# Where the expert's number is read, and when token numbers are made, in the last eleven tiles of a mixture-of-experts kernel

## The chip, the core and the metric

The kernel runs on one core of a Trainium2 chip. The metric is the device time of one execution in microseconds, as the median of several runs. The profile is of one execution.

## What is computed

The model is one gated cross-attention layer followed by a mixture of experts. `x` is 8 x 512 tokens of width 256. The part that matters here is the second one, cut from the reference:

```
logits = einsum('btd,de->bte', layernorm(x), gate_w)      # 8 experts
top_v, top_i = top_k(logits, 2); top_w = softmax(top_v)
for e in range(8):
    h = gelu(xf @ w1[e] + b1[e])                          # 256 -> 1024, exact gelu
    out = out + comb[:, e] * (h @ w2[e] + b2[e])          # 1024 -> 256
x = x + tanh(g_ffn) * out
```

Each token goes to two of the eight experts, so which rows an expert sees is known only when the kernel runs.

## The kernel before

The rows of the tokens are first sorted into one queue per expert in DRAM. The work is then cut into 39 tiles (`N_TILES`): 32 full ones of 256 rows (`N_FULL`) and seven narrow ones of 128 rows, numbers 32 to 38, for what is left over in the experts' queues. Small tables that VectorE makes at run time hold, for each tile, the number of its expert (`expert_of`) and its place in the queue. The weights of all experts lie in the on-chip memory, split into a high and a low bf16 part (`w1_split`, `w2_split`).

The first six tiles (`EARLY`) are interleaved with the last batch of the attention, in an order written out by hand. The rest is run by `over_tiles`: tiles 6 and 7 written out, tiles 8 to 27 in a hardware loop of two tiles a turn, tiles 28 to 38 written out again. `i` is a Python integer in a written-out tile and a register in the loop; `s` is the buffer of two that the tile uses.

Every engine has its own program, kept in step by semaphores. For one tile:

- SyncE (`load`) brings the rows of tile i + 2.
- TensorE first transposes tile i + 1 (`turn`, line 2548), then does layer 1 of tile i (`all_layer1`, line 2562: 48 matmuls over three products of high and low parts), then layer 2 of tile i - 1 (`all_layer2`, line 2578: 48 matmuls in four pieces for a full tile, 24 in two pieces for a narrow one). There is one accumulator for layer 2 (the program's `ps_y`, named `ps_o` in the profile), so layer 2 of tile i - 1 waits until VectorE has added the bias of tile i - 2 out of it (`y_biased`); it also waits for `h_lo_ready`.
- ScalarE casts the transposed rows (`split_x`) and applies gelu (`gelu`).
- VectorE takes the rows' tails, weights and low parts (`prepare`, `low`) and then does `finish` for tile i - 1: bias added into `y` (line 2534), then multiplied by the row's weight (line 2537).
- GpSimd (`add`) waits until the add of tile i - 1 has landed and until `y` is weighted, makes the token numbers of the tile (`token_f`, line 2469, and `token_at`, line 2471), and issues the indirect DMA that adds the rows of `y` to the output (line 2473), one for each 128 rows.

The number of the tile's expert is read from memory into a register of the engine's sequencer by `load_expert` (line 2424), and the address of each weight block is worked out from it in registers. TensorE calls it in `all_layer1` and again in `all_layer2`; VectorE in `prepare` and in `finish`, there behind the waits:

```
dve.wait_ge(y_summed, i + 1)
if not first(i, 2):
    after_add(dve, i - 2, early)
e = load_expert(dve, i)
```

Of the kernel before, what the change touches and what calls it, by code (L numbers as in the profile page):

```python
# [3 lines left out]
P = 128  # L4
# [20 lines left out]
N_FULL, N_HALF = 2 * B * L // TILE, E - 1  # L25
N_TILES, N_ENTRIES = N_FULL + N_HALF, N_FULL + N_HALF + 2
# [7 lines left out]
EARLY = 6  # L34
# [3 lines left out]
F32, BF16, I32, U32 = (mybir.dt.float32, mybir.dt.bfloat16, mybir.dt.int32, mybir.dt.uint32)  # L38
# [188 lines left out]
def program(nc, x, ctx_t, g, wq_t, wkv_t, wc_t, gate_w, w1, b1_t, w2, b2, out):  # L227
# [11 lines left out]
    with ExitStack() as whole:  # L239
# [45 lines left out]
        general_select(nc, k, sem, sb, ps, general[0])  # L285
        general_attend(nc, k, sem, sb, ps, general[1])
        experts(nc, k, sem, sb, ps, pipeline, general)


# [2098 lines left out]
def experts(nc, k, sem, sb, ps, pipeline, general):  # L2388
    with ExitStack() as own:
# [8 lines left out]
        weight = sb(own, "weight", [P, N_TILES, 2])  # L2398
        part_a, part_b = sb(own, "part_a", [P, 2]), sb(own, "part_b", [P, 2])
        bias = [sb(own, f"bias{s}", [P, FC]) for s in range(2)]  # L2400
        token_f, token_at = sb(own, "token_f", [P, 2]), sb(own, "token_at", [P, 2], I32)
        x_hi, x_lo, ps_x, ps_h, ps_y = k.x_hi, k.x_lo, k.ps_x, k.ps_h, k.ps_y

        bias_loaded, x_turned = sem("bias_loaded"), sem("x_turned")
# [1 line left out]
        tail_taken, x_hi_ready, x_lo_ready = sem("tail_taken"), sem("x_hi_ready"), sem("x_lo_ready")  # L2406
        h_ready, gelu_done, h_lo_ready = sem("h_ready"), sem("gelu_done"), sem("h_lo_ready")
        y_summed, y_biased, y_weighted, added = sem("y_summed"), sem("y_biased"), sem("y_weighted"), sem("added")
# [4 lines left out]
                    y_biased, y_weighted)  # L2413

        all_met, pads_placed = sem("all_met"), k.pads_placed

        def first(i, n=1):
            return isinstance(i, int) and i < n

        def slot_of(i, s):  # L2420
            return (i % 2, i // 2) if isinstance(i, int) else s

        def load_expert(engine, i):
            return engine.value_load(k.expert_of[0:1, bass.ds(i, 1)], min_val=0, max_val=E - 1)

        def width(i):
            return P if isinstance(i, int) and i >= N_FULL else TILE

        def loaded(i, s, half):
            again = isinstance(i, int) and i >= N_FULL - 1 and s == (N_FULL - 1) % 2  # L2430
            return row_loaded[s], 16 * (half + (2 if again else 1))
# [21 lines left out]
        def after_add(engine, i, early):  # L2453
            if isinstance(i, int) and i < EARLY - 1:
                done, before = early
                engine.wait_ge(done, before + 32 * (i + 1))
            elif width(i) == P:
                engine.wait_ge(added, 32 * (N_FULL + 1 - EARLY) + 16 * (i + 1 - N_FULL))
            else:
                engine.wait_ge(added, 32 * (i + 2 - EARLY))  # L2460

        def add(pool, chain, i, at=None, early=(added_early, 0)):
            g = nc.gpsimd
            s, _ = slot_of(i, at)
            some = width(i) // P
            if not first(i):
                after_add(pool, i - 1, early)
            pool.wait_ge(y_weighted, i + 1)
            chain.then(g.tensor_tensor(token_f[:, 0:some], tails[:, bass.ds(i, 1), 0:some, 3].rearrange("p a s -> p (a s)"),  # L2469
                                       k.ones_f[:, 0:some], ALU.mult))  # L2470
            chain.then(g.tensor_copy(token_at[:, 0:some], token_f[:, 0:some]))  # L2471
            for t in range(some):
                pool.indirect_dma_start(k.out_rows, bass.IndirectOffsetOnAxis(ap=token_at[:, t:t + 1], axis=0),  # L2473
                                        y[s][:, t, :], None, bounds_check=B * L - 1, oob_is_err=False,
                                        compute_op=ALU.add).then_inc(early[0] if first(i, EARLY - 1) else added, 16)

# [46 lines left out]
        def finish(dve, i, at=None, early=(added_early, 0)):  # L2523
            v = nc.vector
            s, _ = slot_of(i, at)
            if first(i):
                dve.wait_ge(bias_loaded, 32)
            dve.wait_ge(y_summed, i + 1)
            if not first(i, 2):
                after_add(dve, i - 2, early)  # L2530
            e = load_expert(dve, i)
            some = width(i) // P
            b2_own = b2_all[:, bass.ds(e, 1), :].to_broadcast([P, some, D])
            v.tensor_tensor(y[s][:, 0:some], ps_y[:, 0:some], b2_own, ALU.add).then_inc(y_biased, 1)  # L2534
            dve.wait_ge(y_biased, i + 1)
            for t in range(some):
                last = v.tensor_scalar(y[s][:, t, :], y[s][:, t, :],  # L2537
                                       weight[:, bass.ds(i, 1), t:t + 1].rearrange("p a s -> p (a s)"), None, ALU.mult)
            last.then_inc(y_weighted, 1)

        def turn(pe, i, at=None):
            s, half = slot_of(i, at)
            pe.wait_ge(*loaded(i, s, half))
            if not first(i):
                pe.wait_ge(x_lo_ready, i)
            for kt in range(KT):
                for t in range(width(i) // P):
                    last = nc.tensor.transpose(ps_x[:, kt, t * P:(t + 1) * P], xg[s][:, t, kt * P:(kt + 1) * P], k.ident[:])  # L2548
            last.then_inc(x_turned, 1)
# [17 lines left out]
        def layer2(pe, i, n, at=None, e=None):  # L2567
            s, _ = slot_of(i, at)
            e = load_expert(pe, i) if e is None else e
            if n == 0:  # L2570
                pe.wait_ge(h_lo_ready, PAIRS * (i + 1))
                if not first(i):
                    pe.wait_ge(y_biased, i)
            t, some = n // 2, range((n % 2) * FC // 2, (n % 2 + 1) * FC // 2)
            token = slice(t * P, (t + 1) * P)
            terms = [(f, hs, part) for f in some for hs, part in ((h_hi, 0), (h_hi, 1), (h_lo, 0))]
            for q, (f, hs, part) in enumerate(terms):
                last = nc.tensor.matmul(ps_y[:, t, :], hs[s][:, f, token],  # L2578
                                        k.w2_split[:, bass.ds(e, 1), part, f, :].rearrange("p a d -> p (a d)"),
                                        start=(n % 2 == 0 and q == 0), stop=(n % 2 == 1 and q == len(terms) - 1))  # L2580
            if n == 2 * width(i) // P - 1:
                last.then_inc(y_summed, 1)
# [1 line left out]
        k.load_expert, k.load, k.load_bias, k.add, k.split_x, k.gelu = load_expert, load, load_bias, add, split_x, gelu  # L2584
        k.prepare, k.low, k.finish, k.turn, k.layer1, k.layer2 = prepare, low, finish, turn, layer1, layer2

        def all_layer1(pe, i, at=None):
            e = load_expert(pe, i)
            for n in range(PAIRS):
                layer1(pe, i, n, at, e)  # L2590

        def all_layer2(pe, i, at=None):
            e = load_expert(pe, i)
            for n in range(2 * width(i) // P):
                layer2(pe, i, n, at, e)

        def meet(engine, n):
            engine.drain().then_inc(all_met, 1)
            engine.wait_ge(all_met, 5 * n)

        def cleared(engine):
            engine.drain().then_inc(all_met, 1)
            engine.wait_ge(all_met, 15 + 4 + len(in_tiles))
            engine.drain()
# [18 lines left out]
        def over_tiles(engine, body):  # L2623

            body(EARLY, EARLY // 2, 0, True, True)
            body(EARLY + 1, EARLY // 2, 1, True, True)
            with engine.Fori(EARLY // 2 + 1, N_FULL // 2 - 2) as j:
                body(2 * j, j, 0, True, True)
                body(2 * j + 1, j, 1, True, True)
            for i in range(N_FULL - 4, N_TILES):  # L2630
                body(i, i // 2, i % 2, i + 1 < N_TILES, i + 2 < N_TILES)

        def after_early(i, n=0):
            return not (isinstance(i, int) and i <= EARLY + n)
# [115 lines left out]
        @block.tensor  # L2750
        def _(pe):
            def early():
                cleared(pe)
                pe.wait_ge(k.tables_ready, 5)
                for i in range(EARLY):
                    turn(pe, i)
                    all_layer1(pe, i)
                    if i:
                        all_layer2(pe, i - 1)

            pipeline.pe(pe)
            in_general(pe, general[0].pe, general[1].pe, nothing, early)

            def body(i, half, s, more, two_more):
                if more:
                    turn(pe, i + 1, (1 - s, half + s))
                all_layer1(pe, i, (s, half))
                if after_early(i):
                    all_layer2(pe, i - 1, (1 - s, None))

            turn(pe, EARLY)
            all_layer2(pe, EARLY - 1)
            over_tiles(pe, body)
            all_layer2(pe, N_TILES - 1)


# [29 lines left out]
```

## Time and profile before

| what | us |
|---|---|
| runs (3): lowest, median, highest | 923.81, 924.6, 925.47 |
| the profiled execution, its own time | 923.9 |
| its span, first to last instruction | 922.1 |
| layer 2 of tile 31, start | 855.43 |
| layer 2 of tile 37, start | 904.96 |
| layer 2 of tile 38, start | 909.29 |
| last indirect DMA, start | 916.16 |

Times inside the profile count from the start of the span. A name like L2578 is a line of the kernel, PE is TensorE, PEld its weight loads, DVE VectorE, ACT ScalarE, POOL GpSimd; an engine name with a q behind it (PEldq, DVEq, POOLq) is a step that the engine's sequencer does itself. An arrow in square brackets names what the view takes for the end of the idle time before the instruction.

### The profile page before, as it was taken

What the parts mean: (1) busy time and instruction counts of PE and PEld (TensorE: products, weight loads), DVE (VectorE), ACT (ScalarE), POOL (GpSimd) and SP (SyncE); (2) the same over time, 40 slices, a digit from 0 to 9 for tenths busy, and PEclk for the clock granted to TensorE, in tenths of its full rate; (3) what the DMA queues carried; (4) which work ended last, traced back from release to release, by engine and by line L of the source; (5) the groups of instructions that cost most, each with busy time, mean ns of one, the idle gap of its engine ahead of it and who ended that gap; (6) DMA issues with size and microseconds to landing.
All of it is one profiled execution on the core that took longest, in us unless ns stands there. A gap on an engine that the chain in (4) does not pass through costs nothing.

```text
span 922.1 us, 20046 instructions
## 1 busy us (share of the span) xinstructions
PE 801.9 (87%) x6326; PEld 547.1 (59%) x6327; DVE 521.0 (56%) x1582; ACT 370.3 (40%) x772; POOL 427.6 (46%) x469
## 2 busy tenths in 40 slices
PE   3785899989897998888778868999999999999994
PEld 1333344435353443443347657899888888899773
DVE  4585576667767567776444873544444544444441
ACT  1222363735435363566653612433333333333331
POOL 4596363755666546443614753333333333333322
PEclk9886899979899898989989989999999999999998
DMA  5554333353624334224425342322222333322300
GB/s 173 129 122 139 60 92 80 117 104 93 128 95 109 64 114 105 69 70 136 138 88 160 54 127 46 59 47 46 44 46 44 55 53 50 48 42 36 44 12 1
DMA packets 62798, 74.64 MB, mean 81 GB/s; under 512 B 6401, under 2 KB 56449, under 8 KB 62593
## 3 DMA queue, kind: packets, MB, share of 16 engines
q1 hardware_dynamic: 49424, 56.74, 24.0%
q0 software_dynamic: 13296, 16.92, 10.7%
q8 instruction: 42, 0.69, 0.3%
q14 instruction: 36, 0.29, 0.1%
HBM read 46.75 MB, written 27.55 MB: 81 GB/s over the span
## 4 chain that ended last, share of the span: by engine, by line
PE 66%; DVE 12%; ACT 6%; issue 6%; POOL 5%; DMA 3%; DVEq 1%; SPq 1%; ACTq 0%; POOLq 0%
PE ps_o L2578 20%; PE ps_d L2562 9%; PE ps_a L2562 9%; PE ps_d L1237 6%; PE ps_o L1317 5%; PE ps_d L1280 3%; PE ps_e L1212 3%; PE ps_e L1342 3%; PE ps_a L1300 2%; PE ps_e L1195 2%; DVE row_max L987 2%; PE ps_r L2548 1%; ACT prob L805 1%; ACT rows L827 1%; PE ps_a L1304 1%
## 5 line engine op out<-in xcount | busy, mean ns | idle before, releaser
L2578 PE MATMUL ps_o<-w_split,hidden 128*128 x1136 | 192.2, 276 | 13.4 <-DVE y L2534 8.4
L805 ACT ACTIVATE prob<-ps_a 128x512 f32<-128x512 f32 x192 | 112.9, 603 | 188.0 <-PE ps_a L1300 109.8
L987 DVE TENSOR_REDUCE row_max<-ps_d 128x2 f32<-128x384 f32 x237 | 127.8, 551 | 58.8 <-PE ps_d L1280 57.4
L2578 PE MATMUL ps_o<-w_split,h_lo 128*128 x568 | 156.6, 276 | 0.0
L2473 POOL DMA_INDIRECT out<-y,token_at x71 | 118.5, 1669 | 42.3 <-POOL token_at L2471 30.9
L2578 PEld LDWEIGHTS ps_o<-w_split,hidden 128*128 128x128 bf16 x1136 | 112.1, 99 | 30.2 <-issue 15.3
L2520 DVE TENSOR_TENSOR h_lo<-hidden 128x512 bf16<-128x512 f32 (+1 forms) x156 | 101.0, 686 | 25.5 <-ACT hidden L2489 24.7
L2534 DVE TENSOR_TENSOR y<-ps_o,b_all 128x512 f32<-128x512 f32 (+1 forms) x39 | 25.1, 644 | 155.6 <-PE ps_o L2578 148.7
L1280 PE MATMUL ps_d<-k_st,w_split 96*128 96x192 bf16 x474 | 84.4, 267 | 26.4 <-DVE row_max L987 19.8
L2562 PE MATMUL ps_a<-x_hi,w_split 128*128 128x256 bf16 (+1 forms) x624 | 104.4, 265 | 0.0
L2562 PE MATMUL ps_d<-x_hi,w_split 128*128 128x256 bf16 (+1 forms) x624 | 103.6, 264 | 0.1
L2469 POOL TENSOR_TENSOR token_f<-tails,ones_f 128x2 f32<-128x2 f32 (+1 forms) x39 | 7.7, 197 | 206.0 <-DVE y L2537 203.7
L706 POOL TENSOR_TENSOR w_split<-w_stage,w_split 128x1024 bf16<-128x1024 f32 x32 | 68.9, 2177 | 54.8 <-ACT w_split L849 54.8
L2480 ACT CAST x_hi<-ps_r 128x512 bf16<-128x512 f32 (+1 forms) x39 | 21.4, 548 | 168.6 <-PE ps_r L2548 168.6
L2489 ACT ACTIVATE hidden<-ps_d,bias 128x256 f32<-128x256 f32 (+1 forms) x156 | 62.4, 452 | 62.1 <-PE ps_d L2562 62.1
L1280 PEld LDWEIGHTS ps_d<-k_st,w_split 96*128 96x128 bf16 x474 | 39.7, 103 | 78.2 <-DVE row_max L987 31.9
L2562 PE MATMUL ps_a<-x_lo,w_split 128*128 128x256 bf16 (+1 forms) x312 | 81.9, 263 | 0.0
L1317 PE MATMUL ps_o<-prob,v_st 128*32 128x512 f32 x512 | 76.8, 675 | 5.5 <-issue 4.1
L2562 PE MATMUL ps_d<-x_lo,w_split 128*128 128x256 bf16 (+1 forms) x312 | 81.4, 263 | 0.0
L2489 ACT ACTIVATE hidden<-ps_a,bias 128x256 f32<-128x256 f32 (+1 forms) x156 | 62.4, 452 | 35.5 <-PE ps_a L2562 35.5
L700 POOL DMA_INDIRECT queue<-rows,slot x64 | 63.9, 999 | 19.4 <-issue 17.1
L2562 PEld LDWEIGHTS ps_a<-x_hi,w_split 128*128 x624 | 60.7, 97 | 9.4 <-issue 1.2
(242 smaller groups left out, 1307.1 us busy)
## 6 DMA issues: line engine op xcount, KB each, us to landing
w_stage<-w SPq DMA_DIRECT2D x32, 512.0 KB, 4.5
xg<-queue SPq DMA_DIRECT2D x31, 260.0 KB, 2.9
w_split<-q_split SPq DMA_DIRECT2D x24, 256.0 KB, 8.0
x_in<-x SPq DMA_DIRECT2D x8, 512.0 KB, 4.3
ctx_sb<-ctx_t SPq DMA_DIRECT2D x8, 512.0 KB, 3.9
x<-x SPq DMA_DIRECT2D x8, 512.0 KB, 4.3
q_split<-q_hl SPq DMA_DIRECT2D x16, 256.0 KB, 3.4
out<-x SPq DMA_DIRECT2D x8, 512.0 KB, 5.0
```

The source lines that it names most:

```text
L700: pool.indirect_dma_start(k.queue[:], bass.IndirectOffsetOnAxis(ap=slot[:, t, c:c + 1], axis=0), rows[:, t, :], None).then_inc(scattered, 16)
L706: g.tensor_tensor(lo, stage, hi, ALU.subtract).then_inc(w_lo, 1)
L805: a.activation(prob[n % 2][:, j, :], ps_a[i % 2][:], ACT.Exp, scale=SCALE).then_inc(exp_ready, 1)
L987: v.tensor_reduce(row_max[:, t, 2 * pair:2 * pair + 2], bank[:, 0:2 * SLOTS].rearrange("p (h r) -> p h r", h=2), AX.X, ALU.max).then_inc(m ...
L1237: last = t_.matmul(ps_da[n][:], q_t[:, kt, t * P:(t + 1) * P], ctx_sb[:, kt, :], start=(kt == 0), stop=(kt == KT - 1))
L1280: last = t_.matmul(ps_da[n][:, c * SLOTS:(c + 1) * SLOTS], q_st[m % 3][0:ROW_MAX, 2 * pair + c, t * P:(t + 1) * P], k_st[0:ROW_MAX, m % 3, ...
L1317: last = t_.matmul(ps_o[j * VW:(j + 1) * VW, :], values, probs, start=(key_tile == 0), stop=(key_tile == SLOT_TILES - 1))
L2473: pool.indirect_dma_start(k.out_rows, bass.IndirectOffsetOnAxis(ap=token_at[:, t:t + 1], axis=0), y[s][:, t, :], None, bounds_check=B * L ...
L2489: last = nc.scalar.activation(hidden[s][:, f, 0:width(i)], ps_h[n][:, c, 0:width(i)], ACT.Gelu, bias=bias[s][:, f:f + 1])
L2520: nc.vector.tensor_tensor(h_lo[s][:, both, tokens], hidden[s][:, both, tokens], h_hi[s][:, both, tokens], ALU.subtract).then_inc(h_lo_read ...
L2562: last = nc.tensor.matmul(ps_h[n][:, c, 0:width(i)], k.w1_split[:, bass.ds(e, 1), part, kt, f].rearrange("p a f -> p (a f)"), xs[s][:, kt, ...
L2578: last = nc.tensor.matmul(ps_y[:, t, :], hs[s][:, f, token], k.w2_split[:, bass.ds(e, 1), part, f, :].rearrange("p a d -> p (a d)"), start ...
```

## The change

It concerns `finish`, `add`, `all_layer1`, `all_layer2` and TensorE's loop body. In the eleven tiles that are written out at the end (i from `LOOPED` = 28 on), TensorE keeps the expert's number of a tile in a register for both layers, and reads the one of tile i + 1 inside layer 2 of tile i - 1, ahead of its last piece. GpSimd makes the token numbers of these tiles as soon as `prepare` has taken the tails, ahead of the two waits, and `token_at` has two buffers. In `finish`, for all tiles, the load of the expert's number stands ahead of the waits.

```
-        token_f, token_at = sb(own, "token_f", [P, 2]), sb(own, "token_at", [P, 2], I32)
+        token_f, token_at = sb(own, "token_f", [P, 2]), [sb(own, f"token_at{s}", [P, 2], I32) for s in range(2)]
...
+        LOOPED = N_FULL - 4
...
+        def wait_rows(pool, i, early):
+            if not first(i):
+                after_add(pool, i - 1, early)
+            pool.wait_ge(y_weighted, i + 1)
+
         def add(pool, chain, i, at=None, early=(added_early, 0)):
...
-            if not first(i):
-                after_add(pool, i - 1, early)
-            pool.wait_ge(y_weighted, i + 1)
+            ahead = isinstance(i, int) and i >= LOOPED
+            if ahead:
+                pool.wait_ge(tail_taken, i + 1)
+            else:
+                wait_rows(pool, i, early)
             chain.then(g.tensor_tensor(token_f[:, 0:some], tails[:, bass.ds(i, 1), 0:some, 3].rearrange("p a s -> p (a s)"),
                                        k.ones_f[:, 0:some], ALU.mult))
-            chain.then(g.tensor_copy(token_at[:, 0:some], token_f[:, 0:some]))
+            chain.then(g.tensor_copy(token_at[s][:, 0:some], token_f[:, 0:some]))
+            if ahead:
+                wait_rows(pool, i, early)
...
         def finish(dve, i, at=None, early=(added_early, 0)):
...
+            e = load_expert(dve, i)
             dve.wait_ge(y_summed, i + 1)
             if not first(i, 2):
                 after_add(dve, i - 2, early)
-            e = load_expert(dve, i)
...
-        def all_layer2(pe, i, at=None):
-            e = load_expert(pe, i)
-            for n in range(2 * width(i) // P):
+        def all_layer2(pe, i, at=None, e=None, ahead=None):
+            e, following = load_expert(pe, i) if e is None else e, None
+            pieces = 2 * width(i) // P
+            for n in range(pieces):
+                if n == pieces - 1 and ahead is not None:
+                    following = load_expert(pe, ahead)
                 layer2(pe, i, n, at, e)
+            return following
...
             def body(i, half, s, more, two_more):
                 if more:
                     turn(pe, i + 1, (1 - s, half + s))
+                if isinstance(i, int) and i >= LOOPED:
+                    if i not in expert:
+                        expert[i] = load_expert(pe, i)
+                    all_layer1(pe, i, (s, half), expert[i])
+                    following = all_layer2(pe, i - 1, (1 - s, None), expert.get(i - 1), i + 1 if more else None)
+                    if more:
+                        expert[i + 1] = following
+                    return
                 all_layer1(pe, i, (s, half))
                 if after_early(i):
                     all_layer2(pe, i - 1, (1 - s, None))
...
-            all_layer2(pe, N_TILES - 1)
+            all_layer2(pe, N_TILES - 1, None, expert[N_TILES - 1])
```

`all_layer1` takes the number as an argument in the same way and loads it only where none is given.

## Rows read from the trace of the kernel before

**Rows 1.** Windows: busy us of each engine, clock, DMA (full tiles, a narrow tile).
```profile
786.00:841.00 55.00, 55.00 (x506) 49.52 (x505) 26.06 (x65) 19.70 (x45) 18.98 (x20) 1.00 0.29 44
876.03:884.10 8.07, 7.34 (x75) 5.87 (x75) 3.38 (x12) 2.86 (x9) 1.93 (x3) 1.00 0.11 22
```

**Rows 2.** Chain of waits from 840 us: start, us, what.
```profile
846.22 5.25 PE ps_o L2578 x48
...
872.96 2.81 PE ps_o L2578 x24
...
897.16 2.81 PE ps_o L2578 x24
...
904.96 2.89 PE ps_o L2578 x24
```

**Rows 3.** Timeline of TensorE, first and last matmul of a layer 1, then layer 2.
```profile
868.08 0.23 PE L2562 MATMUL ps_d<-x_hi,w_split 128*128 128x128 bf16 x1
...
872.07 0.23 PE L2562 MATMUL ps_a<-x_hi,w_split 128*128 128x128 bf16 x1
872.96 0.41 PE L2578 MATMUL ps_o<-w_split,hidden 128*128 x2 [0.66 <-DVE h_lo L2520]
```

**Rows 4.** Timeline of VectorE, low parts of tile 33.
```profile
864.08 1.42 DVE L2520 TENSOR_TENSOR h_lo<-hidden 128x256 bf16<-128x256 f32 x4
```

**Rows 5.** Lines 2424 and 2573, 871.9 to 873.0: ns min/median/max, first and last start.
```profile
L2424 PEldq TENSOR_LOAD <-expert_of x1: 297/297/297, 872.1 to 872.1; - x1
L2424 PEldq FUSED_REGOPS  x1: 151/151/151, 872.4 to 872.4; - x1
L2424 PEldq SEQ_ASSERT  x1: 18/18/18, 872.7 to 872.7; - x1
...
L2573 PEldq EVENT_SEMAPHORE  x1: 51/51/51, 872.7 to 872.7; - x1
```

**Rows 6.** Line 2562, 868.0 to 872.3, one narrow layer 1.
```profile
L2562 PEldq FUSED_REGOPS  x32: 46/46/46, 868.0 to 872.0; - x32
```

**Rows 7.** Line 2545 at 849 us, and TensorE's timeline at layer 1 of tile 32.
```profile
L2545 PEldq EVENT_SEMAPHORE  x1: 51/51/51, 849.3 to 849.3; - x1
...
851.51 0.22 PE L2562 MATMUL ps_d<-x_hi,w_split 128*128 128x128 bf16 x1
851.57 0.22 PE L2562 MATMUL ps_d<-x_lo,w_split 128*128 128x128 bf16 x1
```

**Rows 8.** Lines 2424 and 2534 and timelines, from layer 2 of tile 37 on.
```profile
L2424 DVEq TENSOR_LOAD <-expert_of x1: 304/304/304, 907.9 to 907.9; - x1
...
L2534 DVEq FUSED_REGOPS  x1: 57/57/57, 908.5 to 908.5; - x1
...
908.60 0.42 DVE L2534 TENSOR_TENSOR y<-ps_o,b_all 128x256 f32<-128x256 f32 x1 [3.18 <-PE ps_o L2578]
...
909.29 0.41 PE L2578 MATMUL ps_o<-w_split,hidden 128*128 x2 [1.45 <-DVE y L2534]
```

**Rows 9.** GpSimd's timeline, line 2473 and the landing, the last two adds.
```profile
910.78 1.56 POOL L2473 DMA_INDIRECT out<-y,token_at  x1 [0.78 <-POOL token_at L2471]
...
914.19 0.18 POOL L2469 TENSOR_TENSOR token_f<-tails,ones_f 128x1 f32<-128x1 f32 x1 [1.85 <-DVE y L2537]
...
916.16 1.56 POOL L2473 DMA_INDIRECT out<-y,token_at  x1 [1.54 <-POOL token_at L2471]
...
L2473 POOLq MOVE  x1: 29/29/29, 914.6 to 914.6; - x1
...
DMA to landing us min/median/max: 2.7/2.7/2.7
```

**Rows 10.** Timelines of VectorE and TensorE in the last batch of the attention.
```profile
504.84 0.69 DVE L2534 TENSOR_TENSOR y<-ps_o,b_all 128x512 f32<-128x512 f32 x1 [2.23 <-issue]
...
512.32 1.09 PE L1195 MATMUL ps_e<-ident,rows 128*128 128x128 f32 x8 [1.63 <-ACT rows L827]
...
513.02 5.97 DVE L2520 TENSOR_TENSOR h_lo<-hidden 128x512 bf16<-128x512 f32 x1 [2.26 <-ACT hidden L2489]
```

More of the change, by code:

```diff
@@ L2465, in add @@
             some = width(i) // P
-            if not first(i):
-                after_add(pool, i - 1, early)
-            pool.wait_ge(y_weighted, i + 1)
+            ahead = isinstance(i, int) and i >= LOOPED
[3 more added lines that the diff above has]
+                wait_rows(pool, i, early)
             chain.then(g.tensor_tensor(token_f[:, 0:some], tails[:, bass.ds(i, 1), 0:some, 3].rearrange("p a s -> p (a s)"),
                                        k.ones_f[:, 0:some], ALU.mult))
-            chain.then(g.tensor_copy(token_at[:, 0:some], token_f[:, 0:some]))
+            chain.then(g.tensor_copy(token_at[s][:, 0:some], token_f[:, 0:some]))
+            if ahead:
+                wait_rows(pool, i, early)
             for t in range(some):
-                pool.indirect_dma_start(k.out_rows, bass.IndirectOffsetOnAxis(ap=token_at[:, t:t + 1], axis=0),
+                pool.indirect_dma_start(k.out_rows, bass.IndirectOffsetOnAxis(ap=token_at[s][:, t:t + 1], axis=0),
                                         y[s][:, t, :], None, bounds_check=B * L - 1, oob_is_err=False,
@@ L2585, in experts, with all_layer1 @@
         k.prepare, k.low, k.finish, k.turn, k.layer1, k.layer2 = prepare, low, finish, turn, layer1, layer2
-        def all_layer1(pe, i, at=None):
-            e = load_expert(pe, i)
+        def all_layer1(pe, i, at=None, e=None):
+            e = load_expert(pe, i) if e is None else e
             for n in range(PAIRS):
                 layer1(pe, i, n, at, e)
-        def all_layer2(pe, i, at=None):
-            e = load_expert(pe, i)
-            for n in range(2 * width(i) // P):
+        def all_layer2(pe, i, at=None, e=None, ahead=None):
[4 more added lines that the diff above has]
+                    following = load_expert(pe, ahead)
                 layer2(pe, i, n, at, e)
+            return following
         def meet(engine, n):
@@ L2626, in over_tiles @@
             body(EARLY + 1, EARLY // 2, 1, True, True)
-            with engine.Fori(EARLY // 2 + 1, N_FULL // 2 - 2) as j:
+            with engine.Fori(EARLY // 2 + 1, LOOPED // 2) as j:
                 body(2 * j, j, 0, True, True)
                 body(2 * j + 1, j, 1, True, True)
-            for i in range(N_FULL - 4, N_TILES):
+            for i in range(LOOPED, N_TILES):
                 body(i, i // 2, i % 2, i + 1 < N_TILES, i + 2 < N_TILES)
@@ L2769, in body @@
                     all_layer2(pe, i - 1, (1 - s, None))
+            expert = {}
             turn(pe, EARLY)
```

## The prediction

> **What bounds the kernel now.** I read the stage table first, for where TensorE is short of work. In the looped tiles it is busy all of the time (55.00 of 55.00 us); in one narrow tile near the end it has 7.34 of 8.07 us, at clock 1.00 in both [rows 1]. So the expert tiles up to 31 are bound by matmuls, and nothing that this change saves there can show; the seven narrow tiles (32 to 38) and the end after them are another matter. The chain of waits gives their rhythm: layer 2 of a narrow tile starts at 872.96 and, three tiles on, at 897.16, so 8.07 us a tile, and the last that follows a layer 1 starts at 904.96 [rows 2].
>
> The timeline shows one hole in each such tile. The last layer 1 matmul starts at 872.07, the first of layer 2 at 872.96, with 0.66 us idle that the view puts down to `h_lo` [rows 3]. That name can't be right: `layer2(i - 1)` waits for the `h_lo` of tile i - 1, and for 33 those four subtractions lie at 864.08 to 865.50 [rows 4], 7 us earlier. What does lie in the hole is the sequencer's own work. The line view of `load_expert` has a TENSOR_LOAD (297 ns), register arithmetic (151 ns) and an assertion (18 ns) from 872.1, and the next step, the wait of line 2573, comes at 872.7 [rows 5].
>
> The matmuls of a narrow layer 1 don't cover it, because they are not limited by TensorE either. 48 of them take from 868.08 to 872.07, 0.085 us each [rows 3], though the array passes them at 0.055 us when they are already queued (851.51, 851.57 [rows 7]). Beside them stand 32 register steps in 4.0 us, 0.13 us apart [rows 6]: each new weight address is worked out in a register, two per three matmuls. So in narrow tiles the sequencer is the bound, and its two loads per tile count whole.
>
> **The change part by part.**
>
> *TensorE, a load removed.* From first to first the hole is 0.89 us (872.07 to 872.96). What stays is one register step (0.13) and one wait step, of at least its 0.05 us and at most another 0.13 [rows 5, 6]; the load is then 0.63 to 0.71 us, and I take 0.65. Below it can't be than the 0.47 that its three steps add up to.
>
> Each tile now has one load (that of i + 1, in `layer2(i - 1)` ahead of its last piece) where it had two. Loads that stop standing between layer 1 of i and layer 2 of i - 1: i = 32 to 38, seven. 7 x 0.65 = 4.55 us. An eighth, in front of layer 2 of tile 38, is worth nothing: that one waits for `y_biased` (1.45 us idle [rows 8]).
>
> *TensorE, the load that stays and moves.* In a narrow layer 2 a matmul takes 0.109 us of the array (5.25 us for 48 [rows 2]) and 0.085 us of the sequencer, so after the first 12 the queue leads by 0.29 us; a load of 0.65 there leaves TensorE idle for about 0.36 us, and layer 2 grows from 2.81 to some 3.2 us. That is no extra cost, since the sequencer's time per tile is what counts, and the load in front of layer 1 is gone in exchange: 8.07 - 0.65 = 7.42 us a tile. In full tiles the load sits before the fourth piece, behind a long lead: at 849.3 the sequencer is already at the wait of the next `turn` while the array is in layer 2 until 851.47, 1.9 us or 17 matmuls behind [rows 2, 7]. Without that lead each would cost 0.65.
>
> The same lead gives a little more at the start. The load for tile 32 is now in that covered stretch instead of in front of layer 1 of 32, which later runs dry and is held by the sequencer. The bounds are 0 and 0.65; I take 0.25, in the lower half, since 17 matmuls may be all that the queue holds. TensorE's part: 4.55 + 0.25 = 4.8 us (4.4 to 5.6).
>
> *VectorE, `finish`.* The load (304 ns, then register work) begins at 907.9 only after `y_summed`; the address step of the addition comes at 908.5, the addition at 908.60 [rows 8]. Moved ahead of the wait it leaves the address step alone: 0.6 us (0.52 of steps to 0.70). Where does it count? In looped and in most narrow tiles nowhere: TensorE uses `ps_y` again only a layer 1 later. It counts twice at the end: layer 2 of 38 can't start before `y` of 37 has left `ps_y` (909.29), and the last addition stands in the end itself. 1.2 us.
>
> *GpSimd, the token numbers.* After the last wait: `token_f` 914.19, cast, the MOVE that opens the DMA at 914.6, the DMA at 916.16 [rows 9]. Made ahead, the two operations go: 914.6 - 914.19 = 0.4 at least; if the DMA began at the wait, 1.97 at most. MOVE to DMA is the DMA's own preparation and stays, so 0.5. Behind the new wait for `tail_taken` only this tile's own DMA is queued, and `prepare` signals it a whole body earlier. The second `token_at` keeps the running DMA's numbers from being overwritten; it costs nothing. What is late next is the landing of add 37, for which add 38 waits: 2.7 us after 910.78, at 913.5, now 0.7 before the 914.19 [rows 9]. It moves by 0.6 + 0.5 relative to layer 2 of 37, the last rows by 1.2; it stays in time by some 0.5.
>
> *VectorE before the tiles.* `finish(0)` at 504.84 idles 2.23 us, its load among it. The rows of the last batch pass behind it to ScalarE, and TensorE waits 1.63 us for them at 512.32 [rows 10]. 0 to 0.9 us could come forward; ScalarE has its own work until about then, and I take 0.3. All other `finish` loads are covered by matmuls.
>
> Sum: 4.8 + 1.2 + 0.5 + 0.3 = 6.8 us. From the profiled execution's 923.9 us (922.1 of span, 1.8 around it) that is 917.1. The median of the runs is 0.7 above it, inside their spread, so I add half: 917.4 us.
>
> **A rule set against the rows.** The profile shows no matmul dispatched in the 0.6 us from TENSOR_LOAD to the next step [rows 5]. The Trainium skill (Advanced Engine Details and Errata, Sequencer and Instruction Queues) says otherwise: while a control instruction executes, other engine instructions can be read and queued. By that rule the loads would hold nothing up, the hole would have another reason, and the change would gain only its 2.0 us outside TensorE; by the rows it gains 6.8. The trace doesn't agree for this load, so I follow the rows and keep the other as the first rival.
>
> **The rivals.**
>
> 1. The wait, not the load, sets the start of layer 2, as the timeline names it. For it: the label [rows 3]. Against it: 864.08 [rows 4]. Then 1.2 + 0.5 + 0.3 remain: 921.9, with the half added 922.2. Chance 0.06.
>
> 2. The load inside layer 2 is hidden whole, because matmuls there are long. It would spare 0.65 more in each of the five narrow layers 2 that carry one (32 to 36), 3.25 us: 914.1. Against it: 24 x 0.085 + 0.65 = 2.69 of sequencer, just over the 2.62 that the array needs, and the next layer 1 finds no lead. Chance 0.06.
>
> 3. An earlier `finish` moves VectorE against GpSimd in the last batch. One subtraction there took 5.97 us (513.02 [rows 10]), where four of half its size took 1.42 together [rows 4], so some 0.7 each at its size. Another such meeting costs up to 5.3 us: 917.4 to 922.7. Chance 0.06.
>
> 4. Slower: keeping the number in a register costs a further register step for each address. A narrow tile has 32 + 16 of them, about 310 in the sequencer-bound stretch; the gain is gone at 6.8 / 310 = 0.022 us each, and even the shortest such step has 0.046 us [rows 6]. That would be +14 us less 6.8: about 932. Nothing in the diff asks for more addresses, so 0.04.
>
> **How the numbers follow.** The forecast has 0.78 and by its terms' bounds reaches from 915 (the last DMA's and the first batch's full gains, TensorE at 5.6) to 919 (TensorE at 4.4, nothing from the first batch, the median a full 0.7 up). Letting in half of rivals 2 and 3 gives 914.9 to 919.8 for 8 in 10. No change means within 0.2%, 1.85 us, which is about what a measurement of this kernel can tell: rival 1 sits on that edge, and a meeting of rival 3 can reach it. Faster 0.91, same 0.05, slower 0.04.
>
> **What would show it.** Layer 1 to layer 2 without the 0.66 us hole (some 0.25 between starts); narrow layers 2 of 3.2 us with an idle piece in the middle; 7.4 us a tile; the layer 2 of 37 starting near 900; one TENSOR_LOAD of TensorE per tile instead of two; 0.85 instead of 1.45 us before layer 2 of 38; `token_f` long before `y` and the last DMA about 6.5 us earlier. The prediction is wrong if layer 2 still starts 0.6 us late, if 0.085 us per matmul changes, or if the tiles begin later than before.

## The result and the profile after

The changed kernel takes 916.75 us (median of 4 runs, 915.18 to 918.29), against 924.2 us for the kernel before beside it: 0.9916 [0.9903, 0.9928] of its time. The forecast was 917.4 us, range 914.9 to 919.8. The profiled execution took 915.18 us, span 913.4, which is 8.7 less than the profiled one of before. In the changed file `load_expert` is line 2426, layer 1 is line 2573, layer 2 is line 2589, the turn line 2559, the last additions 2545 and 2548, the token numbers 2478 and 2480, the adds 2484.

The windows over the first narrow layer 2 with the layers 1 around it, and over one narrow tile (columns as in [rows 1]), say where the change lies:

```profile
861.00:869.00 8.00, 7.82 (x90) 6.39 (x87) 4.88 (x20) 3.86 (x13) 4.10 (x5) 1.00 0.39 60
869.36:876.73 7.37, 7.18 (x76) 5.70 (x75) 3.41 (x13) 2.89 (x10) 3.29 (x6) 1.00 0.11 22
```

The narrow tile takes 7.37 us instead of 8.07, with TensorE's clock at 1.00 as before and nearly the same busy time (7.18 against 7.34): what went is idle time. The chain of waits shows how layer 2 now runs (start, us, what):

```profile
862.16 1.50 PE ps_o L2589 x12
863.65 0.18 issue
863.84 1.50 PE ps_o L2589 x12
...
869.36 1.50 PE ps_o L2589 x12
870.86 0.15 issue
871.01 1.63 PE ps_o L2589 x12
...
891.29 1.50 PE ps_o L2589 x12
...
898.34 2.88 PE ps_o L2589 x24
```

A layer 2 that was one piece [rows 2] is now two of 12 matmuls with an idle piece between them, where the moved load stands. Layer 2 of 37, whose start was 904.96, starts at 898.34. The timeline of TensorE has the two places themselves, the joint of layer 1 and layer 2 and the middle of layer 2, and the last layer 2:

```profile
869.13 0.23 PE L2573 MATMUL ps_a<-x_hi,w_split 128*128 128x128 bf16 x1
869.36 0.41 PE L2589 MATMUL ps_o<-w_split,hidden 128*128 x2
...
870.59 0.27 PE L2589 MATMUL ps_o<-w_split,h_lo 128*128 x1
871.01 0.54 PE L2589 MATMUL ps_o<-w_split,hidden 128*128 x2
...
902.02 0.41 PE L2589 MATMUL ps_o<-w_split,hidden 128*128 x2 [0.82 <-DVE y L2545]
```

Last matmul of layer 1 to first of layer 2: 0.23 us, where [rows 3] has 0.89 and 0.66 idle. `h_lo` is no longer named. In the middle, 0.42 us from start to start where two neighbours have 0.11. The one load of TensorE in this tile lies exactly there, in the line view of `load_expert`:

```profile
L2426 PEldq TENSOR_LOAD <-expert_of x1: 297/297/297, 870.3 to 870.3; - x1
...
L2426 PEldq FUSED_REGOPS  x1: 151/151/151, 870.6 to 870.6; - x1
...
L2426 PEldq SEQ_ASSERT  x1: 18/18/18, 870.8 to 870.8; - x1
```

The sequencer reads it at 870.3, ahead of the array, so that only a part of its length shows: 0.31 us more between the two starts (0.42 against 0.11), of which the chain counts 0.15 as idle. At the end, the timelines of GpSimd and (last two lines) VectorE:

```profile
903.03 1.56 POOL L2484 DMA_INDIRECT out<-y,token_at  x1 [4.55 <-remote]
904.07 0.73 POOL L2478 TENSOR_TENSOR token_f<-tails,ones_f 128x1 f32<-128x1 f32 x1
904.87 0.18 POOL L2480 CAST token_at<-token_f 128x1 int32<-128x1 f32 x1
907.41 1.56 POOL L2484 DMA_INDIRECT out<-y,token_at  x1 [2.36 <-remote]
...
904.97 0.42 DVE L2545 TENSOR_TENSOR y<-ps_o,b_all 128x256 f32<-128x256 f32 x1 [2.81 <-PE ps_o L2589]
905.43 0.35 DVE L2548 TENSOR_SCALAR y<-y,weight 128x256 f32<-128x256 f32 x1
```

The last token numbers are made at 904.07, in the time of layer 2 of 38, and TensorE waits 0.82 us for `y` of 37 instead of 1.45 [rows 8].

Starts from the timelines divide the 8.75 us of span in three. Layer 2 of 30 starts at 845.27 (before 846.05): 0.78. From there to layer 2 of 37 it is 53.07 us (58.91): 5.84. From layer 2 of 37 to the end of the span it is 15.05 us (17.18): 2.13.

### The profile page after: what moved, and what is told of

It reads as the page before. It is cut to its first block, busy times and chain, and to the rows that moved or that the text cites. A ratio compares the mean times of both kernels' runs of the same rounds, so it can differ in the third digit from the quotient of the medians.

```text
span 913.4 us, 20012 instructions
## 1 busy us (share of the span) xinstructions
PE 798.9 (87%) x6326; PEld 545.7 (60%) x6327; DVE 523.2 (57%) x1582; ACT 370.6 (41%) x772; POOL 426.5 (47%) x469
## 4 chain that ended last, share of the span: by engine, by line
PE 68%; DVE 11%; ACT 6%; issue 6%; POOL 4%; DMA 3%; SPq 1%; DVEq 0%; another core or an unknown queue 0%; ACTq 0%; POOLq 0%
PE ps_o L2589 20%; PE ps_d L2573 10%; PE ps_a L2573 9%; PE ps_d L1237 6%; PE ps_o L1317 5%; PE ps_d L1280 3%; PE ps_e L1212 3%; PE ps_e L1342 3%; PE ps_a L1300 2%; DVE row_max L987 2%; PE ps_e L1195 2%; PE ps_r L2559 2%; ACT prob L805 1%; PE ps_a L1304 1%; ACT rows L827 1%
## 5 line engine op out<-in xcount | busy, mean ns | idle before, releaser
L2478 POOL TENSOR_TENSOR token_f<-tails,ones_f 128x2 f32<-128x2 f32 (+1 forms) x39 | 14.2, 364 | 155.3 <-DVE y L2548 155.3
```

## The experiments

All stand beside runs of the kernel before on the same chip (medians 924.2 to 925.6 us), and each ratio is to those beside it. Every one computes the whole result; the added loads of three of them read a number that nothing uses. "30 to 37" is the time from the first matmul of layer 2 of 30 to that of 37 in the profiled execution, "37 to end" from there to the end of its span, "tile" a third of the time from layer 2 of 33 to that of 36.

| Kernel | median us | ratio to before | 30 to 37 | tile | 37 to end |
|---|---|---|---|---|---|
| before | 924.2 | 1 | 58.91 | 8.07 | 17.18 |
| after | 916.75 | 0.9916 [0.9903, 0.9928] | 53.07 | 7.31 | 15.05 |
| again_all | 916.66 | 0.9912 [0.9899, 0.9925] | 53.09 | 7.32 | 15.06 |
| e1_pe_only | 918.77 | 0.9936 [0.9923, 0.9950] | 53.31 | 7.31 | 17.14 |
| e2_dve_only | 923.48 | 0.9983 [0.9973, 0.9992] | 59.09 | 8.19 | 15.94 |
| e3_pool_only | 924.62 | 0.9998 [0.9987, 1.0009] | 58.93 | 8.12 | 16.70 |
| e4_one_more_load | 922.38 | 0.9968 [0.9950, 0.9985] | 58.28 | 8.08 | 15.01 |
| e5_load_first | 917.38 | 0.9904 [0.9878, 0.9931] | 54.05 | 7.37 | 15.01 |
| e6_all_numbers_early | 913.96 | 0.9868 [0.9838, 0.9898] | 50.04 | 6.70 | 15.00 |
| e7_two_more_loads | 926.59 | 1.0019 [1.0007, 1.0030] | 62.77 | 8.68 | 15.01 |
| e8_load_mid_layer1 | 920.49 | 0.9954 [0.9938, 0.9970] | 57.83 | 7.95 | 15.01 |

**again_all** is the changed kernel itself, run beside its three parts.

> The changed kernel once more, in the same rounds as its three parts. Theory: its gain is the sum of theirs, about 5.8 + 2.2 + 0.5 = 8.5 us by the profiles, 7.5 us by the medians so far; if the parts cover each other, the sum of the three is larger than the whole by a microsecond or more.

It repeats 53.1 and 15.06 us to 0.02; only layer 2 of 30 starts elsewhere, at 847.45.

**e1_pe_only**, the changed kernel with VectorE's load and GpSimd's order as before:

```diff
-            ahead = isinstance(i, int) and i >= LOOPED
+            ahead = False
...
-            e = load_expert(dve, i)
             dve.wait_ge(y_summed, i + 1)
             if not first(i, 2):
                 after_add(dve, i - 2, early)
+            e = load_expert(dve, i)
```

> The changed kernel with TensorE's part alone: finish and add are those of the kernel before. Theory (the sequencer's loads stand in the holes): layer 2 of tile 37 starts 5.8 us earlier relative to layer 2 of tile 30, as in the changed kernel, and nothing else moves: 924.2 - 5.8 = 918.4 us, ratio 0.9937. Rival (layer 2 starts when h_lo is there, as the timeline names it): the holes stay, 924 us, ratio 1.000.

The part of TensorE alone brings 5.6 us between 30 and 37, 0.2 less than expected, and this lies in one load: the TENSOR_LOAD inside layer 2 of 36 (at 894.1) took 515 ns in this profile, where about 300 is usual. The end is that of before: the timelines show the old 1.4 us ahead of layer 2 of 38 and the old preparation of the last DMA.

```profile
904.71 0.41 PE L2589 MATMUL ps_o<-w_split,hidden 128*128 x2 [1.43 <-DVE y L2545]
...
911.58 1.56 POOL L2484 DMA_INDIRECT out<-y,token_at  x1 [1.54 <-POOL token_at L2480]
```

**e2_dve_only**, the kernel before with `e = load_expert(dve, i)` ahead of `dve.wait_ge(y_summed, i + 1)` in `finish`, as the change has it.

> The kernel before with VectorE's part alone: in finish the load of the expert's number stands ahead of the waits. Theory: 0.8 us in the last batch of the attention, 0.6 us before layer 2 of tile 38, 0.6 to 1.0 us before the last y: 922.0 us, ratio 0.9977. Rival (the 0.8 us of the last batch was the chance of one execution): 922.8 us, ratio 0.9985. TensorE's holes of 0.66 us stay in both.

```profile
874.59 0.41 PE L2578 MATMUL ps_o<-w_split,hidden 128*128 x2 [0.66 <-DVE h_lo L2520]
...
910.67 0.41 PE L2578 MATMUL ps_o<-w_split,hidden 128*128 x2 [0.83 <-DVE y L2534]
...
912.16 1.56 POOL L2473 DMA_INDIRECT out<-y,token_at  x1 [0.78 <-POOL token_at L2471]
914.96 0.18 POOL L2469 TENSOR_TENSOR token_f<-tails,ones_f 128x1 f32<-128x1 f32 x1 [1.24 <-DMA out<-y,token_at]
```

The hole of the narrow tiles is whole (0.66), the wait ahead of layer 2 of 38 went from 1.45 to 0.83, and 37 to end became 1.24 us shorter. The last line names a new wait: GpSimd is held by the landing of add 37 (912.16 + 2.7 us), no longer by `y` as in [rows 9].

**e3_pool_only**, the changed kernel with `finish` and TensorE as before: `if i...>= LOOPED:` in TensorE's body becomes `if False:`, the last call `all_layer2(pe, N_TILES - 1)`, and `finish` loads behind its waits.

> The changed kernel with GpSimd's part alone: the token numbers of the last eleven tiles are made ahead of the waits, TensorE and finish as before. Theory: only the two operations behind the last wait go, 0.5 us: 923.7 us, ratio 0.9995, same. Rival (the preparation of the DMA goes with them, so that it starts at the wait): 1.97 us, 922.2 us, ratio 0.998.

```profile
910.46 1.56 POOL L2484 DMA_INDIRECT out<-y,token_at  x1 [5.57 <-remote]
911.51 0.73 POOL L2478 TENSOR_TENSOR token_f<-tails,ones_f 128x1 f32<-128x1 f32 x1
...
915.93 1.57 POOL L2484 DMA_INDIRECT out<-y,token_at  x1 [3.44 <-remote]
```

The token numbers are made 4.4 us ahead of their DMA, and the end is 0.48 us shorter. The runs can't tell that from no change (0.9998); the profile can, since the same stretch repeats within 0.06 us where its code is the same (15.00 to 15.06 in seven profiles, 17.14 and 17.18 in e1 and before). By 37 to end the parts of VectorE and GpSimd are worth 1.24 and 0.48, together 2.13: 0.4 more than their sum.

**e4_one_more_load**, the changed kernel with a load between layer 1 and layer 2 of each narrow tile, where before had one:

```diff
                     all_layer1(pe, i, (s, half), expert[i])
+                    if i >= N_FULL:
+                        load_expert(pe, i)
                     following = all_layer2(pe, i - 1, ...
```

> The changed kernel with one more load of the expert's number, whose value nobody uses, between layer 1 and layer 2 of tiles 32 to 38. Theory (a load holds the sequencer, and the sequencer is the bound): the hole of some 0.65 us is back in seven tiles, 7 x 0.64 = 4.5 us more than the changed kernel: 921.2 us, ratio to the kernel before 0.9965. Rival (other instructions are read and queued while the load executes): no more than 0.5 us, 916.8 us, ratio 0.992.

```profile
872.80 0.23 PE L2573 MATMUL ps_a<-x_hi,w_split 128*128 128x128 bf16 x1
873.67 0.41 PE L2589 MATMUL ps_o<-w_split,hidden 128*128 x2 [0.65 <-DVE h_lo L2531]
```

The hole is back within 0.01 us of [rows 3], and with it the label `h_lo`, though nothing but a load was added: the wait that the view names was never the cause. Seven loads cost 5.2 us between 30 and 37, more than the 4.5 expected: 8.08 a tile against 7.31. Part of the excess is again in single loads; the one ahead of layer 2 of 36 has this line, where about 300 ns are usual:

```profile
L2426 PEldq TENSOR_LOAD <-expert_of x1: 497/497/497, 896.9 to 896.9; - x1
```

**e5_load_first**, the load for the next tile ahead of the first piece of layer 2 instead of the last:

```diff
-                if n == pieces - 1 and ahead is not None:
+                if n == 0 and ahead is not None:
```

> The changed kernel with the load inside layer 2 ahead of its first piece instead of its last. Theory (only the sequencer's total counts in a narrow tile): the idle piece of TensorE moves in front of layer 2 and the tile takes as long; only the load in layer 2 of tile 31, which then follows a layer 1 that has run dry, costs some 0.6 us: 917.3 us, ratio 0.9925. Rival (the lead of layer 2's long matmuls hides part of the load where it stands now): 0.3 us more in each of five narrow tiles besides, 918.9 us, ratio 0.994.

The chain of waits has the idle time (with `h_lo`'s name again ahead of it) in front of a layer 2 of one piece:

```profile
870.90 0.44 DVE h_lo L2531
871.34 0.56 issue
871.90 2.81 PE ps_o L2589 x24
...
879.31 1.72 PE ps_o L2589 x14
```

A narrow tile takes 7.37 us, nearly the 7.31 of the changed kernel. So the place of the one load that stays is worth little; that the other is gone is what counts. What the place did cost stands ahead of the full layer 2 of 31, behind a layer 1 that has run dry, as the theory had it: from layer 2 of 30 to that of 31 it is 9.05 us instead of 8.44, and the hole is there in TensorE's timeline:

```profile
855.56 0.41 PE L2589 MATMUL ps_o<-w_split,hidden 128*128 x2 [0.65 <-DVE h_lo L2531]
```

**e6_all_numbers_early**, the changed kernel with all numbers of narrow tiles loaded inside full layers 2, up to three in one, and kept in registers:

```diff
+        AHEAD = {28: {2: 29, 3: 30}, 29: {1: 31, 2: 32, 3: 33},
+                 30: {2: 34, 3: 35}, 31: {2: 36, 3: 37}, 32: {3: 38}}
...
-                if n == pieces - 1 and ahead is not None:
-                    following = load_expert(pe, ahead)
+                if ahead is not None and n in ahead:
+                    expert[ahead[n]] = load_expert(pe, ahead[n])
```

(The key is the tile whose layer 1 runs in that turn, then the piece of layer 2 and the tile whose number is loaded.)

> The changed kernel with the numbers of tiles 29 to 38 all read inside the full layers 2 of tiles 27 to 31, two or three ahead of their later pieces, and kept in registers; none is read in a narrow tile. Theory: the five loads in narrow layers 2 (32 to 36) no longer hold the sequencer, 5 x 0.64 = 3.2 us less than the changed kernel, less what two loads in one full tile uncover (up to 0.6): 913.8 us, ratio to the kernel before 0.9887. Rival (those loads are hidden under layer 2 already): 916.7 us, ratio 0.992.

```profile
870.29 2.82 PE ps_o L2589 x24
...
877.03 2.81 PE ps_o L2589 x24
...
883.73 2.81 PE ps_o L2589 x24
...
890.38 2.81 PE ps_o L2589 x24
```

Layer 2 is one piece again, with no load on either side, and a tile takes 6.70 us: the load that the change left in narrow tiles cost 0.61 each. The three loads inside the full layer 2 of 28 cost nothing: from layer 2 of 28 to that of 29 it is 10.92 us here and in the changed kernel. Between 30 and 37 it brings 3.03 us over the changed kernel. This is the fastest version, 0.9868 of the time before.

**e7_two_more_loads** has a second added load behind that of e4, **e8_load_mid_layer1** one added load in the middle of layer 1 instead:

```diff
             for n in range(PAIRS):
+                if n == PAIRS // 2 and isinstance(i, int) and i >= N_FULL:
+                    load_expert(pe, i)
                 layer1(pe, i, n, at, e)
```

> The kernel after with two extra loads of the expert number, values unused, between layer 1 and layer 2 of each narrow tile (one extra load there cost 0.76 us a tile: 8.07 us where the kernel after has 7.31). Theory A, the load itself holds the sequencer for 0.76 us: the second adds as much, 8.83 us a tile, about 5.3 us over the run with one. Theory B, the load holds it for the 0.64 us that its steps show and the other 0.12 us belong to the pause at this place: 8.71 us a tile, about 4.5 us over the run with one. Rival by which such steps run beside matmuls: no growth, 8.07 us.

> The kernel after with one extra load of the expert number, value unused, in the middle of layer 1 of each narrow tile instead of between layer 1 and layer 2. Theory A (the load costs 0.76 us wherever the sequencer sets the pace): 8.07 us a tile, as in the run with the load between the layers. Theory B (0.12 us of it belong to that place): about 7.95 us a tile. Rival, the matmuls already queued cover part of it here: 7.3 to 7.7 us.

The hole of e7 in TensorE's timeline:

```profile
874.08 0.28 PE L2589 MATMUL ps_o<-w_split,hidden 128*128 x1 [1.45 <-DVE h_lo L2531]
```

and that of e8, inside layer 1, while its layer 2 follows at once:

```profile
868.59 0.23 PE L2573 MATMUL ps_d<-x_hi,w_split 128*128 128x128 bf16 x1
869.36 0.23 PE L2573 MATMUL ps_a<-x_hi,w_split 128*128 128x128 bf16 x1 [0.54 <-issue]
...
871.26 0.23 PE L2573 MATMUL ps_a<-x_hi,w_split 128*128 128x128 bf16 x1
871.49 0.28 PE L2589 MATMUL ps_o<-w_split,hidden 128*128 x1
```

The second load adds 0.60 us a tile (8.68 less 8.08), the one in layer 1 adds 0.64 (7.95 less 7.31). The first half of theory B holds: a load costs 0.60 to 0.64 us wherever the sequencer sets the pace. Its other half, 0.12 us that belong to the joint, isn't shown. At the three joints that the column "tile" spans in e4 the TENSOR_LOADs took 347, 307 and 497 ns, and beside the usual 300 that is 0.08 of the 0.12 us a tile. No place in a narrow tile gave the cover that the rival asked for.

One stretch of e7 shows the bound from the other side. It follows narrow tiles in each of which TensorE sat idle for some 1.5 us, and in it the granted clock was 0.51, the lower of its two levels (1.2 GHz):

```profile
900.40:903.80 3.40, 3.40 (x18) 2.43 (x18) 0.00 (x0) 0.00 (x0) 0.00 (x0) 0.51 0.00 0
```

It lies in layer 2 of 36, which the column "tile" no longer covers. The matmuls start 0.21 us apart there, so this layer 2 takes 4.28 us from first to last start, where those of 34 and 35 take 2.89. The sequencer gets ahead of it, and layer 1 of 38, which comes next, takes 2.69 us instead of the 3.8 of the changed kernel, because its matmuls are queued. So 1.1 of the 1.4 us come back, and 0.3 stay in the 62.77.

## Why the prediction was right, and where its sizes were off

The mechanism stood. That the sequencer bounds the narrow tiles, and that a load counts whole there, was shown by putting loads back (e4, e7, e8) and by taking the last ones out (e6).

**TensorE, 4.8 predicted, 5.84 measured.** Start to start in the timelines, before and after:

| Stretch | before | after | change | predicted |
|---|---|---|---|---|
| joint of layer 1 and layer 2, seven times | 6.26 | 1.71 | -4.55 | -4.55 |
| layers 1 of 32 and 33 | 6.23 | 5.42 | -0.81 | -0.25 |
| layers 2 of 32 to 36 | 13.45 | 15.11 | +1.66 | about +1.8 |
| layers 1 of 34 to 38 and the turns ahead of four of them | 22.03 | 19.88 | -2.15 | about -1.8 |

The joint came out to the hundredth, which is luck: in e2 and e3, whose TensorE is that of before, the seven joints take 6.62 and 6.50 us, with single loads of up to 540 ns, so the profiles give 4.55 to 4.9. Two smaller terms were mis-sized. *The lead of full tiles* was sized at 0.25 in fear that 17 matmuls were all the queue holds. It hides the load whole, and not one but two loads left narrow layers 1 for it, that for 32 and that for 33, which now stands in the full layer 2 of 31; the prediction counted only the first. (Some 0.2 of the 0.81 belong to the one trace of before, where the load at 859.0, that for layer 1 of 33, took 495 ns; in e2 and e3 the two layers take 6.03 and 6.10 us.)

*The moved load* was taken as an even trade: it costs 1.66 us in layer 2 (0.33 each, 0.36 predicted) but gives back 2.15 in front of and inside layer 1. Layer 1 itself became 0.30 us shorter and the turn ahead of it 0.16. This isn't the change of the 0.085 us per matmul that the prediction named as a sign of being wrong: the first twelve matmuls of these layers 1 take 0.78 us instead of 1.06, because some of them are queued by then and pass 0.056 us apart, and from the 13th start to the last it is 3.04 us before and 3.02 after. The trade gives 0.1 us a tile more than layer 2 grew. Counted from step to step of the sequencer, from layer 2 of 33 to that of 36, the loads take 1.31 us a tile before and 0.65 after, an even trade at 0.65 each; the 0.1 lies in the address steps of layer 2 (2.16 and 2.06), some of which come 0.16 to 0.28 us after one another instead of 0.12. Why they do isn't settled.

**GpSimd, 0.5 predicted:** 0.48 (e3). **VectorE, 1.2 predicted:** 1.24 (e2), and this agreement is luck. The prediction took 0.6 us twice, from the rows of tile 37. The wait ahead of layer 2 of 38 did shrink by that (37 to 38: 4.33 us before, 3.68 after). But the last addition starts 3.93 us after layer 2 of 38 in the kernel before, whose line is

```profile
913.22 0.42 DVE L2534 TENSOR_TENSOR y<-ps_o,b_all 128x256 f32<-128x256 f32 x1 [3.81 <-issue]
```

and 2.95 us after it in the changed kernel (902.02 to 904.97) and in e2: 0.98. Why its load costs 0.36 more there than that of tile 37 (0.41 us between address step and addition, in the chain) isn't shown; the line was in the trace of before. VectorE's part is then worth 1.6, and in e2 a late landing takes 0.36 of it back.

**What is late next** was looked for in the right place. The landing of add 37 was expected to stay in time by 0.5 us, with the last rows 1.2 us earlier; they came 1.6 earlier. So with VectorE's part alone the landing is late: in e2 `y` of 38 is weighted at 914.44 (914.08 + 0.35), and GpSimd starts on it at 914.96, 0.52 us later; in the kernel before that step takes 0.16 (914.03 to 914.19), so the landing costs 0.36. GpSimd's part starts add 37 earlier as well, and then the landing (903.03 + 2.7 = 905.73) is in time for the last rows (905.43 + 0.35 = 905.78) by no more than 0.05 us. That is why the two parts together bring 0.4 more than the sum of each alone: 0.65 and 0.98 from VectorE and 0.50 from GpSimd, 2.13 us.

**The last batch of the attention, 0.3 predicted, isn't shown.** The start of layer 2 of 30 is 845.27 in the changed kernel, 0.78 earlier than before, but 847.45 in the second profile of the same kernel. Over all eleven profiles it lies between 845.27 and 847.88, on average 846.6 in the eight with `finish` moved and 846.5 in the three without. The gain, if there is one, is smaller than this scatter, and the changed kernel's profiled execution simply started its tiles early.

Without that scatter the parts are 5.84 + 2.13 = 8.0 us, which is what the ratios say (0.9912 of 925 is 8.1 less). The forecast, with 6.5 for the same parts, was 1.5 low: 0.56 for the lead, 0.49 for the trade, 0.4 for the last addition. With its 0.3 for the last batch it was still 1.2 low (6.8 against 8.0). That the median came within 0.65 us of it is in part luck: the two medians beside each other lie 7.45 apart, those of the repeat 8.5.

**The rivals.** The first (`h_lo` sets the start) falls by e1 and e4. The second (load in layer 2 hidden whole) falls by the idle 0.15 to 0.18 us inside it and by e6, which still found 0.61 a tile in it. The third (a meeting in the last batch) would have cost up to 5.3 us; the latest start of layer 2 of 30 is 1.83 us after that of before (e2, 847.88), so a full one wasn't there, and a small one can't be told from the scatter. The fourth (a register step more per address) falls by the tile of 7.31.

**The rule set against the rows.** The Trainium skill (Advanced Engine Details and Errata, Sequencer and Instruction Queues) says that other engine instructions can be read and queued while a control instruction executes. The runs don't agree for this load: in narrow tiles each one added 0.60 to 0.77 us, and only matmuls that were queued ahead of it ran on. But in every version another step of the sequencer, the address of a weight block, stands between the load and the next matmul, so a matmul that needs no such step was not tried behind a load.

## What to carry to other kernels

When an engine idles a fixed time in every small tile, look at what its sequencer does in that time before believing the wait that the view names; adding the suspected instruction once more settles it in one run. A register load costs nothing where the sequencer is far ahead of the array and its full length where it isn't, so put such loads, all of them, in the last stretch with a long lead, and keep the numbers. And look at the end of the kernel as one race: shortening one leg may only uncover the next, and two edits there can be worth more than their sum.

## What was not expected of the hardware

- The sequencer's lead in a full layer 2 takes in three loads (an estimate of 1.9 us, three times 0.64) without a trace in the time: 10.92 us with three and with one.
- `token_f` takes 0.18 us alone [rows 9] and 0.73 beside the running DMA (904.07); here that is covered.
- In the last add the time from GpSimd's MOVE (905.90) to its DMA (907.41) is 1.5 us, in the add before 0.75 (902.28 to 903.03), in both kernels alike; the chain puts 1.29 of it to another core or an unknown queue. It stays open, and a change of it was not tried.
- The TENSOR_LOAD that reads a tile's number into a register of TensorE's sequencer takes about 300 ns, but single ones took 473 to 561 (in e4 and e8, from layer 2 of 30 on). Where the sequencer is the bound this alone moves a profile by 0.2 us; the cause is open too.
